# Gated cross-attention and mixture of experts on one core: token-major V through memory, softmax on 32x32 squares, half-array attention matmuls, x turned by DMA, four projection banks

## The reference, cut to what matters

```python
def xattn(q, k, v, Wq, bq, Wk, bk, Wv, bv, Wo, bo):       # q = layernorm(x), k = v = context
    Q = (q @ Wq.T + bq).reshape(bs, sl, 16, 64)
    K = (k @ Wk.T + bk).reshape(bs, sl, 16, 64)
    V = (v @ Wv.T + bv).reshape(bs, sl, 16, 64)
    score = jnp.einsum('bshd,bsgd->bshg', Q, K)
    weight = jax.nn.softmax(score, axis=-1)
    attn = jnp.einsum('bshg,bsgd->bshd', weight, V).reshape(bs, sl, 1024)
    return attn @ Wo.T + bo
x = x + tanh(g_xattn) * xattn(layernorm(x), ctx, ctx, ...)
x = x + tanh(g_ffn) * moe(layernorm(x))                   # shared expert, 6 of 64 experts
```

## Time and profile before

| | us |
|---|---|
| three runs | 3426.99, 3423.96, 3425.87 (median 3425.87) |
| profiled execution: its time, its span | 3419.47, 3417.3 |
| attention phase in the trace: first projection matmul to the last attention store | 19.67 to 1480.67 |
| busy in the span: TensorE, VectorE, ScalarE, GpSimd | 3258.9, 2305.6, 1610.8, 1335.0 |
| mean granted TensorE clock | 0.978 of full |

### The profile page before, as it was taken

One profiled execution on the slowest core, in us unless ns is written; L12 is line 12 of the kernel. 1 busy time (PEld: TensorE's weight loads), 2 busy tenths in 40 slices (PEclk: granted clock), 3 DMA queues, 4 the chain that ended last, 5 costly groups with the idle time before them and its releaser, 6 DMA issues. The chain is left out here.

```text
span 3417.3 us, 69728 instructions
## 1 busy us (share of the span) xinstructions
PE 3258.9 (95%) x24064; PEld 2167.4 (63%) x24064; DVE 2305.6 (67%) x3881; ACT 1610.8 (47%) x3324; POOL 1335.0 (39%) x1251
## 2 busy tenths in 40 slices
PE   6999999999999999869999998799999999999996
PEld 5888888888888888634444444455555555555553
DVE  7666666666666666657777776566666666666663
ACT  5555555555555555531111111455555555555552
POOL 1111111111111111024554545466666666666663
PEclk9999999999999999979999999899999999999998
DMA  5011111111111111144445443699999999999997
GB/s 198 26 38 39 39 39 39 39 38 39 38 39 38 39 39 39 38 160 133 140 128 144 132 140 95 206 260 287 266 280 268 283 263 285 269 286 276 286 275 142
DMA packets 272432, 496.25 MB, mean 145 GB/s; under 512 B 95975, under 2 KB 177895, under 8 KB 270160
## 3 DMA queue, kind: packets, MB, share of 16 engines
q0 software_dynamic: 79872, 235.06, 29.4%
q1 hardware_dynamic: 192336, 258.25, 23.0%
HBM read 322.97 MB, written 187.11 MB: 149 GB/s over the span
## 5 line engine op out<-in xcount | busy, mean ns | idle before, releaser
L635 PE MATMUL proj_ps<-ct_hi,wk_wv_hi 128*128 128x256 f16 x2048 | 560.8, 274 | 3.6 <-DVE wk_wv_lo L508 3.5
L637 PE MATMUL proj_ps<-ct_hi,wk_wv_lo 128*128 128x256 f16 x2048 | 559.0, 273 | 0.0
L636 PE MATMUL proj_ps<-ct_lo,wk_wv_hi 128*128 128x256 f16 x2048 | 559.0, 273 | 0.0
L1460 POOL DMA_INDIRECT out<-outs,target x256 | 402.3, 1572 | 298.9 <-ACT outs L1537 239.6
L1558 DVE TENSOR_TENSOR ext_lo<-eturn_ps,ext_hi 128x1024 f16<-128x1024 f32 x254 | 311.2, 1225 | 259.8 <-ACT ext_hi L1507 256.6
L332 POOL TENSOR_TENSOR probs<-probs,rsums 128x512 f32<-128x512 f32 x128 | 133.3, 1041 | 756.9 <-DVE rsums L534 756.9
L1431 POOL DMA_INDIRECT rows<-rows_dram,index x256 | 351.4, 1373 | 121.3 <-issue 85.1
L1507 ACT ACTIVATE ext_hi<-eturn_ps 128x1024 f16<-128x1024 f32 x254 | 260.1, 1024 | 213.1 <-PE eturn_ps L1621 213.0
L407 ACT ACTIVATE probs<-probs,neg_max 128x128 f32<-128x128 f32 x512 | 199.1, 390 | 258.0 <-DVE neg_max L527 258.0
L635 PE MATMUL proj_ps<-xt_hi,wq_wo_hi 128*128 128x256 f16 x1024 | 285.1, 278 | 21.4 <-DVE whole L496 7.3
L1621 PE MATMUL eturn_ps<-ident,rows 128*128 128x128 f32 x2032 | 267.4, 275 | 27.2 <-DMA rows<-rows_dram,index 23.8
(11 more groups left out here) (180 smaller groups left out, 8075.4 us busy)
## 6 DMA issues: line engine op xcount, KB each, us to landing
ew_in<-w_up SPq DMA_DIRECT2D x64, 1024.0 KB, 7.5
ew_in<-w_down SPq DMA_DIRECT2D x64, 512.0 KB, 8.1
x_in<-x SPq DMA_DIRECT2D x16, 1024.0 KB, 6.8
c_in<-ctx_t SPq DMA_DIRECT2D x16, 1024.0 KB, 5.4
attn_dram<-attn SPq DMA_DIRECT2D x16, 1024.0 KB, 4.7
a_in<-attn_dram SPq DMA_DIRECT2D x32, 512.0 KB, 5.2
rx_in<-x SPq DMA_DIRECT2D x32, 512.0 KB, 4.8
rows_dram<-yn SPq DMA_DIRECT2D x32, 512.0 KB, 2.7
```

Source lines behind the costliest of these rows:

```text
L635: pe.matmul(out, wh, hi[:, k, :], start=(k == 0), stop=False)
L636: pe.matmul(out, wh, lo[:, k, :], start=False, stop=False)
L637: last = pe.matmul(out, wl, hi[:, k, :], start=False, stop=(k == KC - 1))
L1460: pool.indirect_dma_start(out=out, out_offset=bass.IndirectOffsetOnAxis(ap=target[:, k:k + 1], axis=0), in_=outs[:, k, :], in_offset=None, ...
```

## The change

- **V**: `project_v` has the context as the stationary operand (128 tokens) and 512 columns of Wv moving, so V comes out with tokens on partitions: 4 units of 24 matmuls, each over two slots. VectorE scales and adds the bias (`keep_v`), ScalarE makes the high part, GpSimd the low part (`split_v`). SyncE stores each unit into `v_dram` (`store_v`) and reads it back as `values` with (token, head) on partitions (`load_values`, two loads a block of 128 partitions x 16 runs of 256 bytes).
- **Attention** by pairs of quads: 4 pairs a block (`PAIR`), each 4 groups of 8 tokens with both halves of the heads. `scores` issues 24 matmuls that alternate between partitions 0-63 and 64-127 as operands; `weigh` issues 24 that alternate between output partitions 0-63 and 64-127.
- **Softmax on squares**: VectorE extracts the four 32x32 diagonal squares of each score matrix with the mask (4 instructions on 32 partitions x 256), takes the maxima; GpSimd subtracts them (`lower`), ScalarE takes one exponential over 128x256, VectorE sums and inverts, GpSimd multiplies, VectorE transposes in 32x32 squares (`dve.transpose`), ScalarE and VectorE write the halves into zeroed 128-wide tiles `probs_t`, 4 instructions each.
- **x** is split first (`split_x`) and then turned by two DMA transposes a block from SyncE (`turn`), in slots 8 and 13.
- **Banks**: four `proj_ps` (`BANKS`), chunk n may start when n-4 is kept.
- Attention is stored four times a block in smaller pieces; routing's load of it has runs of 1 KB, and its two splits write in the permuted order (`by_part`).

```diff
-SLOT = [0, 2, 5, 8, 10, 13, 16, 18]
-ALONE = [0, 2, 4, 6, 8, 10, 12, 14]
-TURN = [12, 20]
+UNITS = QKC + 4
+BANKS = 4
+SQ = 32
+PAIR = [0, 5, 10, 16]
+PAIR_ALONE = [0, 1, 3, 4]
+SUMMED, TURNED, SPLIT, WEIGHED = 1, 2, 3, 5
+XHI = [6, 11]
+XLO = [7, 12]
+XTURN = [8, 13]
...
+                def turn(b, t):                                          # SyncE
+                    sp.wait_ge(x_lo_made, b.times(2, t + 1))
+                    sp.wait_ge(projected, b.times(UNITS, KC - UNITS))
+                    sp.dma_start_transpose(xt[:, :, :, t * P:(t + 1) * P].rearrange("p w k t -> p (w k) t"),
+                                           xw[:].rearrange("p w d -> p (w d)")).then_inc(x_turned[t], 16)
+                def store_v(b, u):
+                    sp.wait_ge(v_lo_made, b.times(4, u + 1))
+                    sp.wait_ge(values_landed[t], b.times(16))
+                    sp.dma_start(v_dram[t * P:(t + 1) * P, c * D:(c + 1) * D], ...).then_inc(v_stored[u], 16)
+                def load_values(a, half):
+                    for u in range(2 * half, 2 * half + 2):
+                        sp.wait_ge(v_stored[u], a.times(16, 16))
+                    sp.wait_ge(attn_made, a.times(2 * NP))
+                    sp.dma_start(values[:, half], v_dram.rearrange("(f j t) (h x) -> f (t h) j x", ...)[half])
                 def step(b, proj, attend, more):
+                    if more and attend:
+                        load_x(b.plus(1))
+                    if attend:
+                        for half in range(2):
+                            load_values(b.plus(-1), half)
                     if more:
                         load_ctx(b.plus(1))
+                    for n in range(CHUNKS):
+                        if proj and n >= QKC and ends(n):
+                            store_v(b, unit(n) - QKC)
+                        if more and n in XTURN:
+                            turn(b.plus(1), XTURN.index(n))
+                        if attend:
+                            for i in due(n, WEIGHED, proj):
+                                store(b.plus(-1), i)
...
+                def maxima(a, i):                                        # VectorE
+                    for k in range(P // SQ):
+                        last = dve.tensor_tensor(square(sc, k)[:, i % 2], square(score_ps, k)[:, :, k * SQ:(k + 1) * SQ],
+                                                 square(mask, k).unsqueeze(1).broadcast_to([SQ, GROUPS, SQ]), ALU.add)
+                    dve.tensor_reduce(neg_max[:, i % 2, :], sc[:, i % 2], AX_X, ALU.max, negate=True)
+                def inverses(a, i):
+                    dve.reduce_sum(sums[:, i % 2, :], sc[:, i % 2], AX_X).then_inc(sum_made, 1)
+                    dve.reciprocal(rsums[:, i % 2, :], sums[:, i % 2, :]).then_inc(rsum_made, 1)
+                def turn_probs(a, i):
+                    dve.transpose(sc_t[:, i % 2]..., sc[:, i % 2]...).then_inc(probs_turned, 1)
+                def split_probs(a, i):
+                    for k in range(P // SQ):
+                        last = dve.tensor_tensor(lo, square(sc_t, k)[:, i % 2], hi, ALU.subtract)
...
+                def scores(a, i):                                        # TensorE; weigh likewise
+                    pe.wait_ge(extracted, a.times(NP, i))
                     for g in range(QUAD):
+                        for x, y in ((0, 0), (0, 1), (1, 0)):
+                            for half in range(2):
+                                made = pe.matmul(score_ps[:, half * QUAD + g, :],
+                                                 group(qk[x][:, a.base % 2, 0], half, i, g),
+                                                 group(qk[y][:, a.base % 2, 1], half, i, g),
+                                                 start=(x == y), stop=(x == 1))
```

More of the change, by code:

```diff
@@ L346, in step @@
                         if attend:
-                            for stage, q in work_after(n - 1, proj):
-                                if stage == "scores":
-                                    divide(b.plus(-1), q)
+                            for i in due(n, SUMMED, proj):
+                                divide(b.plus(-1), i)
+                            for i in due(n, 0, proj):
+                                lower(b.plus(-1), i)
+                        if proj and n >= QKC and ends(n):
+                            split_v(b, unit(n) - QKC)
                 steps(pool, first, step)
@@ L603, in _ @@
             def _(pe):
-                def turn(b, t):
-                    pe.wait_ge(x_normed, b.times(2, t + 1))
-                    pe.wait_ge(xt_lo_made, b.times(2, t))
-                    if b.base >= 2:
-                        ahead = sum(s + 1 <= TURN[t] for s in SLOT)
-                        pe.wait_ge(values_kept, b.plus(-2).times(NQ, ahead))
-                    for k in range(KC):
-                        last = pe.transpose(turn_ps[:, k, :], x_in[:, t, k * P:(k + 1) * P], ident[:])
-                    last.then_inc(x_turned, 1)
                 def project(b, n):
@@ L638, in project, with project_v @@
                     last.then_inc(projected, 1)
-                def rows(q):
-                    half = q % 2
-                    return slice(half * HD, (half + 1) * HD)
-                def group(of, q, g):
-                    t0 = ((q // 2) * QUAD + g) * TOK
-                    return of[rows(q), t0:t0 + TOK, :].rearrange("d t h -> d (t h)")
-                def scores(a, q):
-                    if q == 0:
+                def project_v(b, n):
+                    j = unit(n)
+                    t, c = (j - QKC) // 2, (j - QKC) % 2
+                    if n == QKC and b.register is None and b.base == 0:
+                        pe.wait_ge(w_lo_made, CHUNKS)
+                    if not ends(n):
+                        pe.wait_ge(even_kept, freed(b, j))
+                        pe.wait_ge(odd_kept, freed(b, j))
+                    for k in range(KC // 2 * ends(n), KC // 2 * (1 + ends(n))):
+                        ch, cl = (part[:, k, t * P:(t + 1) * P] for part in (ct_hi, ct_lo))
+                        wh, wl = (w[2][:, k, c * 512:(c + 1) * 512] for w in (w_hi, w_lo))
+                        pe.matmul(proj_ps[j % BANKS][:], ch, wh, start=(k == 0), stop=False)
+                        pe.matmul(proj_ps[j % BANKS][:], ch, wl, start=False, stop=False)
+                        last = pe.matmul(proj_ps[j % BANKS][:], cl, wh, start=False, stop=(k == KC - 1))
+                    if ends(n):
+                        last.then_inc(projected, 1)
@@ L665, in turn_values @@
-                def turn_values(a, q):
-                    pe.wait_ge(values_kept, a.times(NQ, q))
-                    ahead = a.plus(2).times(2, sum(SLOT[q] + 1 > n for n in TURN))
-                    pe.wait_ge(xt_lo_made, min(ahead, 2 * NBLK) if isinstance(ahead, int) else ahead)
-                    pe.sem_inc(apart, 1)
-                    for g in range(QUAD):
-                        last = pe.transpose(values_ps[:, g, :], group(v[:, a.base % 2], q, g), ident[rows(q), rows(q)])
-                    last.then_inc(values_turned, 1)
```

460 lines of the change are left out of this document (249 added, 211 removed).

## The result

| | before | after |
|---|---|---|
| runs, us | 3420.12 to 3426.99, median 3424.91 | 3170.84 to 3172.44, median 3170.93 |
| profiled execution: span | 3417.3 | 3169.2 |
| busy: TensorE, VectorE, ScalarE, GpSimd | 3258.9, 2305.6, 1610.8, 1335.0 | 2986.0, 2214.7, 1346.0, 1372.6 |
| first projection matmul to the last block's attention alone | 19.67 to 1435.31 | 27.28 to 1190.19 |

A forecast was written before the change was run, and what follows sets the result against it. TensorE's own instruction stream was taken to bound attention: -231 us over 15 blocks, +15 new waits, +2 start, -4 last block, -11 tail give -229; from the median 3425.9 that is 3197, rounded to 3198, range 3150 to 3270.

The forecast's parts named there:

- Transposes, shapes, V projection, scores: TensorE per block: transposes of probabilities -4.2, V -3.2, x -1.9; fewer array-shape changes -0.6; V projection -0.2; overlapping score matmuls -3.1 us.
- the division's wait: TensorE's wait for GpSimd's division goes, because weighing comes five slots behind its scores: -0.4 us a block.
- Weighing: Visits of 24 matmuls alternating column halves: 1.12 us taken, between 0.78 overlapped and 1.45 not; -1.8 us a block.
- The stall of some 5 us at each back edge stays: Attention loop: issue waits with a few slow matmuls behind them, about 5 us per back edge, were left unchanged.
- VectorE: The engine late next: 54 us a block beside a block of 71, at 94% in Q/K slots 0 to 15.
- The first rival: VectorE bounds the Q/K slots, deciding from about 0.5 us a small piece; 45 us in all, 3243; chance 0.18.
- The debt: VectorE falls 2 to 3 us behind in the Q/K slots, paid back before the V slots; costed at nothing.
- 1 us a block for waits that appear: Allowance for new waits from thin covers and more engines feeding each visit: 0 to 3 us a block, +15 in all.
- V through memory: V's store and reload land 14 us after block end T, needed at T + 16.6: hidden, 2.6 us to spare.
- Start: First matmul moves from 19.67 to about 27, but weights are awaited until 25 already: +2 us (-2 to +7).
- Tail: Attention alone after the last projections, 45.4 us paced by VectorE and ScalarE, gets shorter: -11 us.
- Last block: VectorE splits output weights while two banks are full; four banks save perhaps 4 of its extra 7 us.

## Why the prediction was right, and where not

The mechanism was right: what left TensorE's stream came off the clock almost in full. By the prediction's own steps:

- *Transposes, shapes, V projection, scores* (12.6 a block, without weighing's 1.8 and the division's wait, 0.4 more): nothing in the trace speaks against a term; an ordinary block took 86.4 before, for 86.0 in the sum. V matmuls start 0.216 apart, scores take 0.77. Each term was start minus start in the rows, so none hung on an assumption.
- *Weighing*, the one term between bounds: taken at 1.12, it is 0.80. That is 0.32 x 4 x 15 = 19 us of the miss. "No row is nearer to one end, so I take the middle" was honest, but rows 5 showed row halves overlapping, and column halves do the same. The rule weighed beside it, that column tiling disables the fast weight load ("TensorEngine Tiling (Array Packing)", Restrictions, in the Trainium skill), gave, as an estimate with the plain load's time that the prediction sets beside it, a visit near 1.4; the measurement, 0.80, decides against it for this shape, and also against the 1.0 from the page's packing factor.
- *"The stall of some 5 us at each back edge stays"* is the step that failed. Its size was right for the kernel before (5.5 at each of five edges), though rows 2 show but half of it: issue waits there are 13.6 us and not 6.6. It was taken as a property of the loop. The kernel with 256-column V shows that it hangs on the V matmuls in front of the edge, and the change had altered just these. Worth 20 us by the two kernels without the loop, 23 by the lengths of their blocks.
- These two make 39 to 42 us. The wait in slot 10 takes some 5 back (1.4 a block for the 1 of the sum), and the blocks missed by 39.
- *VectorE*: 54 predicted, 54.75 measured; extractions 0.42 as priced, and the 32x32 transpose 0.44 (priced at 0.42). Low probabilities average 0.467: from 300 to 1200 us 188 of 200 take 0.40 to 0.42, and twelve, about one a block, 1.28 to 1.39, each while GpSimd makes V's low part. The first rival's point, 0.5 a piece, was not reached, and TensorE waited for no keep. The debt was predicted ("slots 3 to 6: keep, low part, statistics, low probabilities"), and TensorE waited for it, but through the probabilities and not through a bank. The cover considered was the banks'; the low probabilities have two slots, and no bank helps there. Its price fell under "1 us a block for waits that appear" and was 1.4, or 24.8 over the 15 blocks.
- *V through memory*: T + 14 predicted, T + 15.1 measured, needed at T + 16.7. The load takes 8.3 at the median for 4.7 assumed; the queue ahead of it was costed apart at 4. Right in the verdict, by a thinner margin.
- *Start*: the first matmul at "about 27" came at 27.28, and "+2" was 15.5. The step priced x's way in block 0 and stopped at the first matmul. It did not ask what else stands in SyncE's queue ahead of block 1's transposes, which in that block is the weights. Its bound, +7, was too low too.
- *Tail* -11, measured -11.8.
- *Last block* -4: it was 9.2 us longer than an ordinary block before and is 5.5 longer after, so 3.7 came, but not for the reason given. Before, TensorE waited in it for low probabilities (8.1 us) and for no bank, and with two banks instead of four this block is not longer (75.2 for 76.4). That is luck.

By spans the forecast was 19 us above the result: 39 in the blocks and 1 in the tail, less 13 at the start and 8 in routing and experts, which it put at nothing. The other 8 of the 27 are that it counts from a median 6.4 above the profiled execution, and rounding. The misses were independent and of both signs, so the small net error flatters the sum.

## What to carry to other kernels

Walk each engine's queue in order and ask, of each instruction that someone will wait for, what stands ahead of it that nobody waits for: making x's halves two slots later, which took 1.2 us out of VectorE's queue in front of the late instruction and nothing off its work, won 13.5 us, more than taking 4 us a block off the same engine (9.4), of which 0.85 stood in front. When a step moves to another queue, walk that queue in the peeled first pass as well, where it has other work. Look at what each engine does at a loop's back edge, too. And waits don't add: time that one wait gives to a late engine is taken off its next one, so a wait's length is no measure of what its removal brings.

## What the runs showed of the hardware

- Matmuls of 128 columns on the two column halves of the array overlap as fully as those on row halves: 24 in 0.80 us, with 24 loads of 64 columns. Grouped by half, they take 1.27.
- A back edge of this loop costs TensorE some 2.1 us of stall and mostly a stretch at 1.2 GHz behind it if 256-column matmuls (0.109 apart) come before it: 3.8 us in all in the kernel after with such matmuls, 5.5 in the kernel before, where a second stall of 1 to 2 us follows. With 512-column ones (0.216 apart) it is under 1 us.
- Other engines can stall there too, with no releaser shown: ScalarE for 2.9 to 4.6 us in the kernel before, VectorE for 4.8 to 5.2 in the kernel whose result copies ScalarE shares.
- A VectorE instruction on 32 partitions x 256 costs 0.42, as one on 128 x 256 does. About one low-probability instruction a block takes 1.28 to 1.39, always beside GpSimd's work on V.
- 512 KB read in runs of 256 bytes behind other loads landed in 8.3 us at the median (4.8 to 10.0), and its issue held SyncE's queue for up to 5.5 us.
